# Perceiver layer with attention and a 64-expert feed-forward on one core: order of the token copies against the shared expert's first weights, and the queue of two stores

## The reference

```
x = x + cross_attention(layernorm(x), ctx_1024)        # 16 heads, no weights
x = x + self_attention(layernorm(x), wq, wk, wv, wo)   # 16 heads of 32
x = x + ffn(layernorm(x), wg, shared_w1/w2, expert_w1/w2)

def ffn(h):                                   # h: 1024 x 512
    shared = (x1 * silu(x2)) @ shared_w2.T    # x1, x2 = split(h @ shared_w1.T), FFN 1536
    gates  = softmax(h @ wg.T)                # 64 experts
    w, idx = top_k(gates, 8); w /= sum(w)
    # each expert takes at most 160 of its tokens, in token order
    out_e  = (x1 * silu(x2)) @ expert_w2[e].T # for the tokens sent to expert e
    return shared + sum over chosen experts of w * out_e
```

## Time and profile before

| what | value |
|---|---|
| time, median of 3 runs (range) | 2520.09 us (2516.25 to 2521.76) |
| time of the profiled execution | 2523.5 us |
| its span (first to last instruction) | 2521.8 us |
| what lies around the span | 1.7 us |
| mean granted PE clock | 0.981 of 2.4 GHz |
| PE busy | 2417.4 us (96%) |
| block 3 | about 332.1 to 580.2 us |
| block 4 | 580.2 us to the end |

### The profile page before, as it was taken

One profiled execution on the slowest core, in us unless ns is written; L12 is line 12 of the kernel. 1 busy time (PEld: TensorE's weight loads), 2 busy tenths in 40 slices (PEclk: granted clock), 3 DMA queues, 4 the chain that ended last, 5 costly groups with the idle time before them and its releaser, 6 DMA issues.

```text
span 2521.8 us, 54951 instructions
## 1 busy us (share of the span) xinstructions
PE 2417.4 (96%) x22810; PEld 1967.5 (78%) x22810; DVE 1983.5 (79%) x1894; ACT 1688.5 (67%) x2121; POOL 572.0 (23%) x412
## 2 busy tenths in 40 slices
PE   6778989998999999999999999999999999999998
PEld 4567767776888888888888888888888888888886
DVE  7775657656899899998878989988778878877795
ACT  5552343325788788887867878877667767766784
POOL 0000020001233223322322422333222222222221
PEclk9889989998999999999999999999999999999999
DMA  8770032235899999998989999999888888877894
GB/s 232 204 216 1 3 141 101 103 143 227 327 368 375 346 370 374 378 377 329 360 289 326 374 345 367 376 350 357 289 308 323 326 300 324 325 292 273 322 366 134
DMA packets 128531, 715.08 MB, mean 284 GB/s; under 512 B 15488, under 2 KB 23808, under 8 KB 52416
## 3 DMA queue, kind: packets, MB, share of 16 engines
q1 hardware_dynamic: 102048, 665.96, 68.8%
q0 software_dynamic: 26144, 44.06, 8.1%
HBM read 684.46 MB, written 25.49 MB: 282 GB/s over the span
## 4 chain that ended last, share of the span: by engine, by line
PE 76%; issue 0%; DVE 0%; POOL 0%; ACT 0%; ACTq 0%; POOLq 0%; DVEq 0%
PE ps L1592 14%; PE ps L1594 14%; PE ps L1593 14%; PE ps L1670 7%; PE ps L1672 7%; PE ps L1671 7%; PE ps L1623 5%; PE ps L1642 4%; PE ps L1655 3%; PE ps L1580 1%; PE ps L1633 1%; PE ps L1583 0%; DVE e_WL L1483 0%; ACT e_WH L1401 0%; POOL out_rows L1554 0%
## 5 line engine op out<-in xcount | busy, mean ns | idle before, releaser
L1483 DVE TENSOR_TENSOR e_WL<-ring,e_WH 128x2048 fp32r<-128x2048 f32 x462 | 1057.4, 2289 | 231.3 <-ACT e_WH L1401 227.4
L1401 ACT ACTIVATE e_WH<-ring 128x2048 fp32r<-128x2048 f32 x462 | 884.7, 1915 | 110.1 <-PE ps L1594 56.8
L1592 PE MATMUL ps<-e_WH,e_XEh 128*128 128x512 f32 x1536 | 605.0, 394 | 3.6 <-DVE e_XEl L1505 3.6
L1594 PE MATMUL ps<-e_WH,e_XEl 128*128 128x512 f32 x1536 | 599.1, 390 | 0.0
L1593 PE MATMUL ps<-e_WL,e_XEh 128*128 128x512 f32 x1536 | 598.3, 390 | 0.0
L1542 POOL TENSOR_TENSOR e_tick<-e_tick 128x1 f32<-128x1 f32 x126 | 111.9, 888 | 1305.7 <-ACT X L1449 1204.2
L1592 PEld LDWEIGHTS ps<-e_WH,e_XEh 128*128 128x128 f32 x1536 | 288.8, 188 | 62.1 <-DVE e_XEl L1505 4.0
L1594 PEld LDWEIGHTS ps<-e_WH,e_XEl 128*128 128x128 f32 x1536 | 288.6, 188 | 61.2
L1593 PEld LDWEIGHTS ps<-e_WL,e_XEh 128*128 128x128 f32 x1536 | 289.1, 188 | 58.3
L1670 PE MATMUL ps<-e_WH,e_GTh 128*128 128x512 f32 x768 | 319.0, 415 | 1.2 <-issue 1.2
L1672 PE MATMUL ps<-e_WH,e_GTl 128*128 128x512 f32 x768 | 302.1, 393 | 0.0
(11 more groups left out here) (224 smaller groups left out, 3196.2 us busy)
## 6 DMA issues: line engine op xcount, KB each, us to landing
ring<-in_experts SPq DMA_DIRECT2D x462, 1024.0 KB
e_more<-in_experts SPq DMA_DIRECT2D x114, 1024.0 KB
ring<-in_shared SPq DMA_DIRECT2D x12, 1536.0 KB, 6.2
a_K<-in_ctx_k SPq DMA_DIRECT2D x32, 514.0 KB, 5.0
a_V<-in_ctx_v SPq DMA_DIRECT2D x32, 384.0 KB
a_V<-in_ctx_v SPq DMA_DIRECT2D x32, 130.0 KB
X<-in_x SPq DMA_DIRECT2D x4, 512.0 KB, 5.4
xn_scratch<-ring SPq DMA_DIRECT2D x1, 2048.0 KB, 7.3
```

Of the source, the lines that this page charges most:

```text
L1401: act.activation(WH[:, nth % HELD, :], unit(i), ACT.Copy).then_inc(hi_done, 1)
L1483: dve.tensor_tensor(WL[:, at, :], unit(place(kind, n)), WH[:, at, :], ALU.subtract).then_inc(lo_done, 1)
L1592: pe.matmul(dst, h, wh, start=(k == 0), stop=False)
L1594: last = pe.matmul(dst, l, wh, start=False, stop=(k == G - 1))
```

## The change

There are two edits, both in block 3. On ACT `high_up(0)` moves from ahead of the copies of turned tiles to behind the first half's copies and `tokens_high`; `high_up(1)` stays behind the second half's. On DVE `low_up(0)` moves behind the four `tokens_low`. And the two stores of `X` leave POOL's stream for SP's: the first behind the last piece of shared weights and ahead of the experts' units, the second behind the eighth unit, as SP's last DMA of the block.

```diff
@@ block 3, SP
+                def store_rows(half):
+                    tiles = slice(4 * half, 4 * half + 4)
+                    sp.wait_ge(so_added, 4 * half + 4)
+                    sp.dma_start(out_tiles[:, tiles, :], X[:, tiles, :]).then_inc(so_out, 16)
...
                     sp.dma_start(raw(q), shared[q % PAIRS]).then_inc(raw_in[q % LOW], 16)
+                store_rows(0)
                 sp.wait_ge(xs_low, G)
...
                     sp.dma_start(ring[:, at * UNIT:(at + 1) * UNIT], source(i)).then_inc(unit_in[i % R], 16)
+                store_rows(1)
                 sp.wait_ge(zero_out, 32)
@@ block 3, ACT
-                high_up(0)
                 for half in range(2):
                     for t in range(4 * half, 4 * half + 4):
                         copy_turned_tile(t)
                     for k in range(G):
                         tokens_high(k, half)
-                high_up(1)
+                    high_up(half)
@@ block 3, DVE
-                low_up(0)
                 for k in range(G):
                     tokens_low(k)
+                low_up(0)
                 low_up(1)
@@ block 3, POOL
                 for e in range(2):
                     gather(pool, e)
-                for half in range(2):
-                    pool.wait_ge(so_added, 4 * half + 4)
-                    pool.dma_start(out_tiles[:, 4 * half:4 * half + 4, :], X[:, 4 * half:4 * half + 4, :]).then_inc(so_out, 16)
```

## The result

The changed kernel takes 2506.23 us (median of 11 runs, 2503.57 to 2511.5) beside 2520.07 us of the kernel before on the same chip (11 runs, 2514.41 to 2521.76). The ratio is 0.9949, with a 95% interval of 0.9940 to 0.9958: 10.6 to 15.1 us faster, 12.9 us in the middle. A later set of five runs gave 0.9951 (0.9938 to 0.9965). So the direction and most of the size were right, and some 4 us came on top (3.7 by the ratio, 4.7 by the time itself).

A forecast was written before the change was run, and what follows sets the result against it. PE bounds the kernel, busy 2417.4 of 2521.8 us, with gains only in block 3's few waits and its end. -4.6 - 4.6 = -9.2 us from the median of 2520.09 gives 2510.9 us; range 2506.5 to 2517.

The forecast's parts named there:

- the early clock: Rival, chance 0.20: PE's clock rises during block 3's first 16 transposes; total -12.4 to -13 us, time about 2507.5 us.
- Block 4 is a fixed length of PE work: Block 4: PE has almost no gap, so it ends earlier only by as much as its first matmul starts earlier.
- the sign that I had set: Block 4, first row to end, should last 1941.6 us as before, within 2 us; otherwise the whole sum's ground fails.
- Part 1, order: Start of block 3: copies ahead of `high_up(0)` let PE's third turn start at about 336.3 instead of 340.87, -4.6 us.
- The cover named for the moved instructions: Block 3: moved `high_up(0)` and `low_up(0)` keep 3 us or more of slack; otherwise cost at most 1.06 or 1.23 us.
- Part 2: End of block 3: with the second store on SP, block 4 starts at 575.5 instead of 580.16, -4.6 us.
- The rival in which SP is held: End of block 3, chance 0.17: SP waits for its store's landing; store move gives -0.3 to +1.7, time 2515.2 to 2517.2 us.
- My argument against an early rise: Block 3: the first 16 transposes end in logits, as the 8 from 340.87 did, which brought no 2.4 GHz.
- The row of 2.40 us: Block 3, DVE: `low_up(1)` takes 2.40 us beside POOL's subtraction; the pattern, with PE's 1.40 us wait, only moves forward.
- No new wait took the place of the old: Block 4: `e_more` units queue behind the store's 1 MB, first read 23.6 us after issue, so the sum stays.

The follow-up runs named there:

- the store in block 4: Against the kernel before: copies moved as in the change, stores left on POOL, the second issued as POOL's first instruction of block 4; 2504.79 us, ratio 0.9942.
- SP made to wait: Against the changed kernel: SP waits at the end of block 3 until both stores have landed; 2511.03 us, ratio 0.9967.
- 20 fillers: Against the kernel before, order untouched: 20 thrown-away identity transposes on PE between the second and third turn of block 3; 2514.90 us, ratio 0.9985.

## Why the prediction was right, and where it was off

*The range.* It went from 2506.5 to 2517 us. The median of 2506.23 lies 0.3 us below its lower end; the ratio, applied to the 2520.09 from which the forecast was made, gives 2507.2, just inside. So the result is at the end that I had given to the early clock, not in the middle.

*Block 4 is a fixed length of PE work.* Right, though only just by the sign that I had set (1941.6 us, within 2): it took 1939.60. It lasts 1939 to 1942 us in the traces without fillers there. The kernel before was at the upper end: PE had three gaps of 0.9 to 1.2 us there for which the profile shows no releaser, the kernel after one. The seven traces with the stores on SP (1939.6 to 1940.9) and the five with them on POOL (1939.1 to 1941.7) overlap, so I take these 2.0 us as luck in comparing two traces and not as the change's.

*Part 1, order: -4.6 us.* Right. Where the clock doesn't rise early, the first shared matmul comes at 19.71 and 19.28 us instead of 24.11: -4.4 and -4.8, and up to the first logits the difference is 4.6. The cover named for the moved instructions held; DVE's part needed none, since its old order costs nothing.

*Part 2: -4.6 us, with the gap falling from 5.6 to about 1.0.* Right: 5.61 to 0.87 us, -4.74. The reading that POOL's DMA at the end of its block holds the barrier, and the bet that SP's doesn't, are both shown: by the store in block 4 (0.3 us), by SP's 0.87 us with a landing 5.1 us after issue, and by SP made to wait (4.79 us). The rival in which SP is held is out.

*The value for part 1 as a whole* is the step that was mis-sized. I took -4.6 and put the clock's share into a rival with a chance of 0.20. In the new order, with the transposes in a row and no fillers, six traces were taken: early in four (15.56, 15.67, 14.99 and 15.63 us to the first shared matmul), late in two (19.71 and 19.28). Early and late differ by about 4 us, so my estimate of the clock's share is 4 x 4/6 = 2.7 us on average; six executions of five kernels give it only roughly. -4.6 - 2.7 - 4.7 is -12.0, within the measured 10.6 to 15.1. What decides between early and late in one execution is open. My argument against an early rise, that these transposes end in logits as the eight did before, took eight transposes as a sign for sixteen. The Trainium skill's sentence ("TensorE: Matmul & The Clock Gate", Part 1), that activity releases the throttle, pointed the right way, and I gave it less weight than I said it deserved. The traces agree with it in kind (early in four of six), but in the other two PE worked without a gap above 0.22 us for some 13 us at 1.2 GHz. The 8.55 us of the first comparison match the rival's own sum (4.6 + 3.25 + 0.6 = 8.45).

*The row of 2.40 us* for `low_up(1)` I put down to POOL's subtraction beside it, and took it to stay as it was. The first was right, the second wrong. In each of the 14 traces `low_up(1)` and POOL's third subtraction start within 0.11 us of each other, and one of them takes 1.1 us longer: DVE's in the kernel before and with 20 fillers (2.40 and 2.38 us), POOL's in the other 12 (2.28 to 2.37 us, with DVE's at 1.23). What decides which of the two it is isn't settled: both long ones of DVE have the old order, but so have two of the 12. It makes up the 1.2 us in the third column of the table: luck as far as the traces tell, though none of the ten with the new order has the long one, so that the order may shift the odds.

*No new wait took the place of the old.* That the `e_more` loads are issued behind the store in SP's queue cost nothing, as reckoned: the loads were issued at 565.30 and their first reader came at 589.2.

## What to carry to other kernels

Ask of each barrier which engine comes last and what it still holds open: here a store issued by GpSimd as its last work of a block put a gap of 5.6 us there, as long as its landing and a bare barrier; the same store from SyncE 0.9 us, and behind the barrier 0.3. An engine that copies PSUM out for PE should not stand behind a wait for HBM, even one that it could serve first on paper. And when idle time of PE goes, reckon the clock behind it as a term of its own with two values, and look for it in several traces; filling PE's 4.5 us wait in the kernel before with thrown-away transposes until the real work came gained 8.1 us (5.0 to 11.3).

## What the hardware showed that I had not expected

- The same code, in the same order, started the shared expert 15.6 or 19.3 to 19.7 us into the block, only by when the clock fell and rose. In one trace it was still at 2.4 GHz for the block's first transposes (8 in 1.19 us), fell during the last of them and didn't rise again for 13 us, in which PE had no gap above 0.22 us: eight transposes, logits, sixteen transposes.
- The subtractions on DVE and POOL that start within 0.11 us of each other, each with two inputs in SBUF, did not run side by side at full speed: one kept its 1.2 to 1.3 us and the other took 2.3 to 2.4, in all 14 traces.
- Blocks 1 and 2, untouched, ended 325.7 to 332.7 us into the span: 7 us of scatter, half of what the change gains.
- The `raw(0)` load, 1.5 MB issued at the block's start, kept ACT waiting for 6.63, 6.73, 7.58 and 7.97 us in the four traces with the old order. In the old order PE's next transposes stood behind it; in the new one ACT has no wait for it in any trace.
- The block's last store, 1 MB, landed 4.3 us after issue from SP with no load near it, 4.8 from POOL, 5.1 to 5.6 from SP with two loads of 1 MB issued 0.85 us after it, and 10.6 where POOL issued it 0.45 us behind those two. The first store, which the change puts on SP between a piece of 1.5 MB and three units, took 10.4 us (5.8 on POOL before); nothing waited for it.
